# Cross-attention softmax of a transformer block: the maximum subtracted and the sums taken by VectorE

## The reference

```
q = (layernorm(x) @ Wq + bq)            # 16 heads of 32
k = ctx @ Wk + bk ; v = ctx @ Wv + bv   # 77 context rows
scores = einsum('blhd,bshd->bhls', q, k), rows s > l masked with -inf
attn = softmax(scores / sqrt(32), axis=-1)      # over 77
x = x + (attn @ v) @ Wo + bo
x = x + ffn(layernorm(x))
```

## Time and profile before

| | |
|---|---|
| median of 3 runs | 1883.83 us |
| profiled execution, span | 1881.2 us |
| TensorE busy, share of the span | 1540.3 us, 82% |
| VectorE busy | 1155.2 us, 61% |
| ScalarE busy | 724.1 us, 38% |
| POOL busy | 979.3 us, 52% |
| mean granted TensorE clock | 0.911 |

### The profile page before, as it was taken

How to read it: one execution, slowest core, us unless ns; L and a number is a source line. 1 busy time by engine, 2 the same in 40 slices (tenths; PEclk the granted TensorE clock), 3 DMA queues, 4 the chain that set the end, 5 groups by cost and what they waited for, 6 DMA issues and landing times. The chain is left out here.

```text
span 1881.2 us, 30280 instructions
## 1 busy us (share of the span) xinstructions
PE 1540.3 (82%) x9836; PEld 1339.0 (71%) x9837; DVE 1155.2 (61%) x1938; ACT 724.1 (38%) x2225; POOL 979.3 (52%) x926
## 2 busy tenths in 40 slices
PE   7679877797878887798733699888999995989992
PEld 5367766676667776687532588878899985989992
DVE  3257888779887788977758544464344455453445
ACT  2066555465556654566311132232122233232111
POOL 2025667567765676667944235554344356444324
PEclk9889989899989997999765899999999997999996
DMA  7111111111111111110002224233343333233211
GB/s 208 35 44 34 53 38 41 38 60 47 41 47 43 54 42 38 43 50 29 34 34 90 78 61 92 61 82 89 69 90 78 67 80 101 60 90 79 43 23 22
DMA packets 76520, 113.30 MB, mean 60 GB/s; under 512 B 32762, under 2 KB 32762, under 8 KB 76219
## 3 DMA queue, kind: packets, MB, share of 16 engines
q1 hardware_dynamic: 45283, 64.73, 11.5%
q0 software_dynamic: 17920, 29.08, 9.0%
q10 hardware_dynamic: 13144, 17.23, 2.6%
HBM read 84.88 MB, written 39.01 MB: 66 GB/s over the span
## 5 line engine op out<-in xcount | busy, mean ns | idle before, releaser
L1352 PE MATMUL hidden_ps<-gT_hi,w 128*128 128x256 f32 x1920 | 367.2, 292 | 44.8 <-DVE gT_lo L1313 43.8
L1352 PEld LDWEIGHTS hidden_ps<-gT_hi,w 128*128 128x128 f32 x1920 | 315.0, 200 | 48.2 <-issue 47.4
L1381 PE MATMUL expert_ps<-w,hT 128*128 128x512 f32 x1440 | 334.8, 391 | 0.0
L1381 PEld LDWEIGHTS expert_ps<-w,hT 128*128 128x128 f32 x1440 | 268.1, 188 | 54.8
L1162 POOL TENSOR_TENSOR w<-raw,w 128x1024 fp32r<-128x1024 f32 x64 | 151.8, 2385 | 253.0 <-ACT w L1156 253.0
L1352 PE MATMUL hidden_ps<-gT_lo,w 128*128 128x256 f32 x960 | 279.1, 291 | 0.0
L1273 ACT ACTIVATE gl<-hidden_ps 128x512 f32<-128x512 f32 x160 | 94.5, 597 | 466.6 <-PE hidden_ps L1352 411.7
L1297 DVE CAST hT<-gl 128x512 fp32r<-128x512 f32 x160 | 69.0, 431 | 258.6 <-ACT gl L1273 255.6
L1255 POOL DMA_INDIRECT out_dram<-og,idx x80 | 133.6, 1670 | 169.2 <-DVE og L1321 145.5
L468 POOL TENSOR_TENSOR prod_k<-qb,kc 128x128 f32<-128x128 f32 (+7 forms) x128 | 182.7, 1429 | 31.5 <-ACT vs L668 29.0
L1352 PEld LDWEIGHTS hidden_ps<-gT_lo,w 128*128 128x128 f32 x960 | 192.5, 201 | 0.8
(11 more groups left out here) (189 smaller groups left out, 3472.9 us busy)
## 6 DMA issues: line engine op xcount, KB each, us to landing
raw<-L_ffn_moe_w_dram SPq DMA_DIRECT2D x64, 512.0 KB, 3.8
xa<-x_dram SPq DMA_DIRECT2D x32, 256.0 KB, 2.8
xc<-x_dram SPq DMA_DIRECT2D x32, 256.0 KB, 2.6
out_dram<-x ACTq DMA_DIRECT2D x32, 256.0 KB, 2.1
normed_tokens<-z ACTq DMA_DIRECT2D x32, 256.0 KB, 2.3
kb<-context_keys SPq DMA_DIRECT2D x128, 38.5 KB, 2.3
xg<-normed_tokens,idx POOLq DMA_INDIRECT x80, 3.5
out_dram<-og,idx POOLq DMA_INDIRECT x80, 4.9
```

The costliest lines, as they stand in the source:

```text
L1352: last = pe.matmul(pH[:, q, f * W:(f + 1) * W], w1[p][l][:, k, cols], xT[r][:, k, :], start=k == 0 and n == 0, stop=k == KT - 1 and n == 2)
L1381: last = pe.matmul(pY[:, k, :], hT[par][l][:, f, k * P:(k + 1) * P], w2[p][r][:, f, :], start=f == 0 and n == 0, stop=f == FT - 1 and n == 2)
```

## The change

The maximum of each head is now taken with its sign turned, without the scale. VectorE adds it to the scores itself, in two instructions of 616 elements that read PSUM and write `pr` in SBUF. ScalarE then takes exponentials of `pr` in place, two instructions of 616 elements, with scale, without bias and without sums. VectorE sums each half in `share_out` ahead of the reciprocals. TensorE's wait for a free score bank is now one for `shifted` and no longer for the exponentials; the wait for the transposes of the tile before (`pt_mm`) moves from ScalarE to VectorE.

```diff
-                    act.wait_ge(s["nm_done"], t.count(1, 1))
-                    need(act, s["pt_mm"], t.count(4))
-                    need(act, s["rec_done"], t.count(2))
-                    for b in range(4):
-                        for g in range(4):
-                            h = 4 * b + g
-                            e = act.activation(pr[:, b, g, :], psS[:, b, g * SK:(g + 1) * SK], ACT.Exp,
-                                               bias=nm[:, h:h + 1], scale=SCALE, accum_out=den[:, h:h + 1])
-                        e.then_inc(s["exp_done"], 1)
+                    for half in range(2):
+                        act.wait_ge(s["shifted"], t.count(2, half + 1))
+                        shares = pr[:, 2 * half:2 * half + 2, :, :]
+                        act.activation(shares, shares, ACT.Exp, scale=SCALE).then_inc(s["exp_done"], 1)
...
             def share_out(t, half):
                 heads = slice(8 * half, 8 * half + 8)
-                dve.wait_ge(s["exp_done"], t.count(4, 2 * half + 2))
+                dve.wait_ge(s["exp_done"], t.count(2, half + 1))
                 need(dve, s["shared"], t.count(2, half))
+                shares = pr[:, 2 * half:2 * half + 2, :, :].rearrange("p b g k -> p (b g) k")
+                dve.tensor_reduce(den[:, heads], shares, X, ALU.add).then_inc(s["summed"], 1)
+                dve.wait_ge(s["summed"], t.count(2, half + 1))
                 dve.reciprocal(rec[:, heads], den[:, heads]).then_inc(s["rec_done"], 1)
                 dve.wait_ge(s["rec_done"], t.count(2, half + 1))
-                shares = pr[:, 2 * half:2 * half + 2, :, :].rearrange("p b g k -> p (b g) k")
...
-                    need(dve, s["exp_done"], t.count(4))
-                    dve.tensor_reduce(nm[:, :].rearrange("p (b g) -> p b g", b=4), scores, X, ALU.max)\
+                    need(dve, s["shifted"], t.count(2))
+                    dve.tensor_reduce(nm[:, :].rearrange("p (b g) -> p b g", b=4), scores, X, ALU.max, negate=True)\
                        .then_inc(s["mx_done"], 1)
                     dve.wait_ge(s["mx_done"], t.count(1, 1))
-                    dve.tensor_scalar(nm[:, :], nm[:, :], -SCALE, None, ALU.mult).then_inc(s["nm_done"], 1)
+                    need(dve, s["pt_mm"], t.count(4))
+                    for half in range(2):
+                        dve.tensor_tensor(pr[:, 2 * half:2 * half + 2, :, :], scores[:, 2 * half:2 * half + 2, :, :],
+                                          bc(nm[:, 8 * half:8 * half + 8].rearrange("p (b g) -> p b g", b=2), 3,
+                                             [P, 2, 4, SK]), ALU.add).then_inc(s["shifted"], 1)
...
                     for g in range(4):
-                        need(pe, s["exp_done"], t.count(4, g - 3))
+                        need(pe, s["shifted"], t.count(2, g // 2 - 1))
                         last = pe.matmul(psS[:, g, 0:4 * SK], qT[:, g, (t.s % 2) * P:(t.s % 2) * P + P],
                                          kb[:, t.s % 2, g, :], start=True, stop=True)
```

More of the change, by code:

```diff
@@ L364, in build_main @@
         base_out = sem("base_out")
-        names = ("stat_x chain_x rstd_x normed_x xt_mm xt_hi xt_lo q_mm q_evac s_mm masked mx_done nm_done exp_done "
+        names = ("shifted summed stat_x chain_x rstd_x normed_x xt_mm xt_hi xt_lo q_mm q_evac s_mm masked mx_done exp_done "
                  "rec_done shared pt_mm pt_evac pv_mm o_hi o_lo wo_mm bias_x x2_done chain_c stat_c "
```

## The result

The changed kernel takes 1947.45 us (median of 4 runs, 1945.94 to 1950.80) against 1884.43 us: ratio 1.0356, 95% interval 1.0337 to 1.0375. That is 63 us slower; the forecast was 70 us slower, 1954 us.

The account below looks back on a forecast made before the run. VectorE's own queue in half A was taken to bound the 32 steps. Value-sum steps +64 us, clock +8, less 2 of exponential waits, gave +70: 1954 us (60%, 1940 to 1968), range 1925 to 1982.

Parts of the forecast that it names:

- The bound: In 32 steps, VectorE's queue from L789 to L740 is half A; a microsecond more there is one more in the step.
- What POOL covers: VectorE's L706 and L822 wait for POOL's running instruction, hiding or adding time; 17.95 us a round of eight steps.
- depths 5 to 8: Steps whose value sums run over 5 to 8 tiles; first sum hidden by L706's wait for POOL, 0.9 to 1.5 us long.
- depth 3: Step with value sums over three tiles: both collisions with POOL count, +2.9 us.
- Depth 4: Step with value sums over four tiles: a tie with POOL that VectorE was let win, +2.1 us.
- depth 2: Step with value sums over two tiles, the bad one: L706 meets L548, L822 waits for a whole L468; +3.4 us.
- The first four tiles: Tiles before any value sums: 4 times 3.0 us added against 12.0 us of exponential waits gone, 0.
- The clock: Longer TensorE idle in half A lowers half B's clock in one or two more of eight steps: 5 to 10 us.
- Everything adds and collides: Rival, 17%: sums not hidden, depth 4 loses its tie, clock falls in most steps; +101 less 5 us, 1980 us.
- The collisions dissolve: Rival, 15%: L822 comes clear of POOL and the clock holds; +47 us, 1930 us.
- Not slower: Rival, 6%: all stretches of VectorE instructions by POOL go, not L822's alone; +1 us, 1883 us.
- ScalarE as the bound: Rival, 2%: ScalarE is the real bound, 4.8 less 1.6 us in each of 32 steps; -100 us, 1780 us.

Follow-up runs that it names:

- Run 4: Changed kernel with 16 more exponentials of 77 elements a tile on ScalarE, on data nobody reads: 1952.12 us, 853.0 first to last maximum.
- run 3: Kernel before with only ScalarE's share of the change, two exponentials a tile without bias and sums; VectorE's instructions kept: 780.3 us first to last maximum (782.8 before).
- run 5: Changed kernel with the shifts kept on VectorE, but 16 exponentials and their sums back on ScalarE: 1907.17 us, ratio 1.0147.
- run 8: Kernel before with the scale folded into the queries, so that L792 goes; 16 exponentials with bias and sum stay: 1869.92 us, ratio 0.9947.
- run 1: Changed kernel without the sum of the first half, its 8 sums set to 1 once: 819.7 us first to last maximum (843.2 with it).
- run 6: Changed kernel with the reciprocals in PSUM, so the multiplication has one input in SBUF and one in PSUM: 1930.11 us, ratio 1.0266.
- run 7: Changed kernel with 28 unread matmuls ahead of TensorE's transposes of ao, in all steps but those after depth 1: 1921.06 us, ratio 1.0211.
- run 2: Changed kernel without both sums, all set to 1 once: 801.5 us first to last maximum (forecast 803), 1887.76 us in all.
- kernel with a shorter half A: Kernel before with scale folded into the queries, reciprocals in PSUM and layernorm of z2 on ScalarE: 1813.19 us; with idle matmuls added 1811.71 and 1811.06.

## Why the prediction was right

- **The bound** held. A step is half A, VectorE's own queue, and then half B. Run 4, with ScalarE 160 us busier, and run 3, with it 108 us less busy, moved the time by 5 to 10 and by 2.6 us, against the 100 that ScalarE as the bound would give; runs 5 and 8 moved it with VectorE's queue.
- **Costs of the new instructions**, measured and in brackets forecast, us: shift 0.794 (0.79), sum 0.783 (0.79), sign 0 (0), exponential 0.72 (0.8). The starts of the maximum lie 1.95 us further apart in the mean (2 to 3). ScalarE's busy time fell by 105 us and not by 230: I subtracted two columns that overlap, where 32 times 4.8 less 1.4, 109 us, follows from the starts.
- **What POOL covers**: that the first sum is free at depths 5 to 8 is shown by run 1, its cause by run 6. The forecast gave 17.95 us a round of half A, measured were 15.7. Its worst entry is depth 3, +2.9 against +1.5. The step that failed there: I let both new collisions count and did not take off an old one. In the kernel before, the second L706 of that step lasts 2.13 us, as it waits for L468; now L823 meets L468 first and the second multiplication is clear of it. From the timelines, before:

```profile
433.70 0.98 DVE L822 TENSOR_SCALAR z<-h,mvf,rf 128x512 f32<-128x512 f32 x1
...
434.83 2.13 DVE L706 TENSOR_TENSOR pr<-pr,rec 128x616 f32<-128x616 f32 x1
...
434.76 1.54 POOL L468 TENSOR_TENSOR prod_k<-qb,kc 128x640 f32<-128x640 f32 x1 [0.37 <-ACT vs L668]
```

and after:

```profile
455.96 1.27 DVE L823 TENSOR_SCALAR z<-h,mvf,rf 128x512 f32<-128x512 f32 x1
...
458.20 0.80 DVE L703 TENSOR_TENSOR pr<-pr,rec 128x616 f32<-128x616 f32 x1
...
454.83 2.11 POOL L468 TENSOR_TENSOR prod_k<-qb,kc 128x640 f32<-128x640 f32 x1
```

- Depth 4 is the same omission (the second L706 took 2.17 us before) and a lost tie with L548 (the first L703 takes 1.83 us), which nearly cancel. At depth 2 the 0.3 us that L823 was to lose beside L468 did not come (1.15 us after, 1.18 before). At depths 7 and 8 the third round of the kernel before had collisions of its own (16.6 against 15.9 at depth 7), which lowers the mean.
- **The first four tiles**: forecast 0, measured +3.3. Half A of tile 1 grew by 1.5 us, as VectorE, done with its own queue, waits there for TensorE's output projection; half A of tile 3 grew by 1.0 and half B after tile 1 by 0.9. The prediction had the projection's delay hidden; in tile 1 it isn't:

```profile
116.47 0.69 DVE L737 TENSOR_TENSOR x<-ring_ps,xc 128x512 f32<-128x512 f32 x1 [1.44 <-PE ring_ps L421]
```

- **The clock**: forecast 5 to 10, taken at 8. Half B grew by 2.2 and 3.2 us in the two middle rounds, above all after depth 2 (+2.2), the step that I had named; run 7 shows the clock to be the cause there. But it shrank by 4.1 in the first round. The premise that a longer idle of TensorE lowers the clock failed after depth 3: in the second round TensorE idled 4.2 us of the half A before it instead of 2.7, and the clock of half B rose from 0.88 to 1.00. I had counted losses only; what sets the clock from step to step stays open.
- **The sum**, first to last maximum: half A of the tiles with value sums +54.3 (forecast 62), their half B +2.8 (8), the first four tiles +3.3 (0), together +60.3 against 70. The mechanism is the one forecast, and the 10 us too many are the two terms above, 8 in half A and 5 in the clock, less the 3 of the first tiles. The 2.6 us by which the spans differ more than the distances lie outside it, and no run looks into them.
- **The rivals.** Everything adds and collides (1980): refuted by run 1 at depths 5 to 8. Its sum took off 5 us of waits where the prediction itself had 14.9; with these it would have been 1970. The collisions dissolve (1930): they don't, L823 went from 1107 to 1243 ns in the mean. Not slower (1883; its sum gives 1885): refuted by the result, as L703 still takes 1037 ns in the mean. ScalarE as the bound (1780): refuted by runs 3 and 4.

## What to carry to other kernels

Find the engine whose own queue, start to end, makes up the loop, and price a change by what it puts into that queue; what it takes from an engine beside it is worth next to nothing (here 105 us of ScalarE's time for 2.6). Scale, bias and sum in many small ScalarE instructions were the better choice here, where ScalarE had slack, though their number looks bad. In such a queue an instruction that waits for POOL is worth more than its length: moving one operand to PSUM gave 17 us at no other cost, and removing a 0.17 us instruction 9 to 14. The reverse holds too: a sum of 0.8 us put in front of such a wait cost nothing. And a forecast for a whole stage is best checked step by step: the distance of run 2 agreed with a sum of which both terms were wrong.

## What the runs showed of the hardware

- The multiplication with two SBUF inputs waits for POOL's instruction under way, 1037 ns in the mean for 800; with one of the two in PSUM it takes 799 or 800 ns, 64 times out of 64. The new sums, reductions from SBUF (774 to 795 ns), and the shifts, from PSUM and SBUF (786 to 800), are never touched. The Trainium skill ("SBUF — State Buffer", "Who interferes with whom") states the same of two SBUF inputs and of reductions, and run 6 agrees.
- Idle matmuls can pay or not. In the changed kernel they raised the granted clock of half B in the middle rounds, 0.70 to 0.88 after six of the eight depths, to 1.00 after all but one (0.96), and took 26 us off. In the kernel with a shorter half A the same idea gave nothing (1811 against 1813). Where they reached past the end of half A, the transposes behind them came as much later, and at 1.2 GHz the same matmul takes 0.41 us instead of 0.27.
- Removing an instruction can lengthen the loop: without the first sum, half A at depth 8 took 17.42 us instead of 17.05, as the small L802 (L801) now meets POOL's L541 and takes 0.73 us instead of 0.39.
